# GpSimd's scatters and gathers wait for the landing of the two transfers of the tile two in front, not for all behind each eight

## The reference

```
x = x + tanh(g_xattn) * attention(layernorm(x), ctx)      # 16 heads of 16
x = x + tanh(g_ffn) * (moe(xf) + shared(xf))              # xf = layernorm(x)

# moe: 16 experts, 2 for each token
logits = xf @ Wg;  gates = softmax over the 2 largest of logits
y = sum over the 2 chosen e of gate_e * ((silu(xf @ W1[e] + b1[e]) * (xf @ W11[e] + b11[e])) @ W2[e] + b2[e])
# shared: the same form with 1024 hidden columns, for all tokens
z = (silu(xf @ Ws1 + bs1) * (xf @ Ws11 + bs11)) @ Ws2 + bs2
```

## Time and profile before

| | |
|---|---|
| median of 3 runs | 604.57 us (603.31 to 604.68) |
| profiled execution, its own time | 601.22 us |
| its span, first to last instruction | 599.5 us |
| mean granted clock of TensorE | 0.983 |
| busy: PE, DVE, ACT, POOL | 556.3, 355.3, 223.2, 345.9 us |
| the 32 scatters | from 219.84 us on |
| the 32 gathers | from 533.30 us on |

### The profile page before, as it was taken

One profiled execution on the slowest core, in us unless ns is written; L12 is line 12 of the kernel. 1 busy time (PEld: TensorE's weight loads), 2 busy tenths in 40 slices (PEclk: granted clock), 3 DMA queues, 4 the chain that ended last, 5 costly groups with the idle time before them and its releaser, 6 DMA issues.

```text
span 599.5 us, 11874 instructions
## 1 busy us (share of the span) xinstructions
PE 556.3 (93%) x3212; PEld 442.9 (74%) x3213; DVE 355.3 (59%) x856; ACT 223.2 (37%) x756; POOL 345.9 (58%) x294
## 2 busy tenths in 40 slices
PE   5789999999976899988899999999999999999995
PEld 4356666566654788867788888888888888888884
DVE  5559778778746562224555566665555555535685
ACT  0687877777756211120222222222222122232331
POOL 4577899899768546672444674464474460236660
PEclk9899999999988899999999999999999999999998
DMA  7572000001020152232455687557557210012224
GB/s 254 205 295 81 28 27 24 21 26 35 10 80 18 48 226 92 93 108 85 175 188 195 232 297 246 201 199 263 191 192 291 88 53 27 28 60 85 85 80 141
DMA packets 32321, 76.07 MB, mean 127 GB/s; under 512 B 4896, under 2 KB 21408, under 8 KB 29344
## 3 DMA queue, kind: packets, MB, share of 16 engines
q1 hardware_dynamic: 12944, 51.52, 23.9%
q10 hardware_dynamic: 16272, 15.74, 8.4%
q0 software_dynamic: 3072, 8.39, 4.4%
HBM read 54.93 MB, written 18.61 MB: 123 GB/s over the span
## 4 chain that ended last, share of the span: by engine, by line
PE 80%; DVE 6%; POOL 5%; issue 4%; ACT 2%; DMA 1%; another core or an unknown queue 1%; DVEq 0%; SPq 0%; ACTq 0%; POOLq 0%
PE mid L674 14%; PE big L655 7%; PE big L657 7%; PE big L656 7%; PE big L574 5%; PE big L572 5%; PE work L425 4%; PE big L573 4%; PE big L454 4%; PE mid L665 3%; POOL arena L1334 2%; PE last L477 2%; PE mid L465 2%; PE work L440 2%; PE work L591 2%
## 5 line engine op out<-in xcount | busy, mean ns | idle before, releaser
L823 ACT ACTIVATE last<-arena 128x512 f32<-128x512 f32 x47 | 28.3, 602 | 184.0 <-DVE arena L1216 184.0
L758 ACT ACTIVATE arena<-big,nmax 128x128 f32<-128x128 f32 x256 | 90.3, 402 | 7.1 <-DVE nmax L939 7.1
L674 PE MATMUL mid<-dring,arena 128*128 x376 | 88.9, 379 | 0.0
L1216 DVE TENSOR_TENSOR arena<-big,bring 128x512 f32<-128x512 f32 x47 | 32.5, 692 | 89.4 <-PE big L657 89.4
L655 PE MATMUL big<-u_hi,xsT_hi 128*128 x188 | 82.4, 438 | 1.6 <-issue 1.6
L1350 POOL TENSOR_TENSOR u_lo<-arena,u_hi 128x2048 fp32r<-128x2048 f32 x16 | 73.3, 4584 | 1.3
L1334 POOL TENSOR_TENSOR arena<-arena,rinv 128x1024 f32<-128x1024 f32 x32 | 60.7, 1896 | 23.2 <-DVE rinv L947 23.2
L657 PE MATMUL big<-u_hi,xsT_lo 128*128 x188 | 73.7, 392 | 0.0
L674 PEld LDWEIGHTS mid<-dring,arena 128*128 128x128 f32 x376 | 67.8, 190 | 7.4
L656 PE MATMUL big<-u_lo,xsT_hi 128*128 x188 | 73.2, 389 | 0.0
L1431 POOL TENSOR_TENSOR pool_mark<-mhalf 128x1 f32<-128x1 f32 x15 | 2.9, 193 | 106.2 <-PE big L657 89.7
(11 more groups left out here) (157 smaller groups left out, 1169.1 us busy)
## 6 DMA issues: line engine op xcount, KB each, us to landing
arena<-up_w_dram SPq DMA_DIRECT2D x16, 1024.0 KB, 7.6
bring<-expert_bias_dram SPq DMA_DIRECT2D x16, 640.0 KB, 5.3
dring<-down_w_dram SPq DMA_DIRECT2D x18, 512.0 KB, 3.4
sorted_y<-arena ACTq DMA_DIRECT2D x47, 128.0 KB, 1.7
arena<-sorted_x ACTq DMA_DIRECT2D x43, 128.0 KB, 2.1
sorted_x<-dring SPq DMA_DIRECT2D x3, 1536.0 KB, 8.6
dring<-up_w_dram SPq DMA_DIRECT2D x2, 1024.0 KB, 4.8
xf_all<-xfs SPq DMA_DIRECT2D x16, 128.0 KB, 2.0
```

Source lines behind the costliest of these rows:

```text
L674: i = mm(mid[:, 1, 0:D], gT[:, p, c, :], dring[:, slot, c * D:(c + 1) * D], start=(c == 0), stop=(c == HC - 1))
L758: i = nc.scalar.activation(probs[:, u % 2, h, :], big[:, u % 2, h // 4, (h % 4) * CTX:(h % 4 + 1) * CTX], ACT.Exp, bias=nmax[:, u % 2, h:h ...
```

## The change

Scatters: in place of the one semaphore `scattered` there are two, one for the even and one for the odd tiles. Before the two transfers of tile t, from tile 2 on, POOL waits until those of tile t-2 have landed, which is all transfers of that parity so far. The wait behind each eight is gone, and nothing on POOL waits for the last tiles' landing any more. SP and ACT wait for both semaphores at 256. Gathers: the same, with `gathered_even` and `gathered_odd` in place of the four semaphores, and `combine(t)` waits for its own tile (`32 * (t // 2 + 1)` of its parity) in place of its group.

```diff
-        scattered = sem("scattered")
+        scattered_even = sem("scattered_even")
+        scattered_odd = sem("scattered_odd")
+        scattered = (scattered_even, scattered_odd)
...
-        gathered = (gathered_0, gathered_4, gathered_8, gathered_12)
+        gathered_even = sem("gathered_even")
+        gathered_odd = sem("gathered_odd")
+        gathered = (gathered_even, gathered_odd)
...
# SP, and in the same way ACT
-            sp.wait_ge(scattered, 16 * TILES * TOPK)
+            for half in scattered:
+                sp.wait_ge(half, 16 * TILES * TOPK // 2)
...
# DVE, combine(t)
-                dve.wait_ge(gathered[t // GROUP], 32 * GROUP)
+                dve.wait_ge(gathered[t % 2], 16 * TOPK * (t // 2 + 1))
...
# POOL, scatters
             for t in range(TILES):
+                if t >= 2:
+                    pool.wait_ge(scattered[t % 2], 16 * TOPK * (t // 2))
                 for k in range(TOPK):
                     g.indirect_dma_start(out=sorted_x, out_offset=bass.IndirectOffsetOnAxis(ap=pos[:, k, t:t + 1], axis=0),
-                                         in_=xf_all[:, t, :], in_offset=None).then_inc(scattered, 16)
-                if t % GROUP == GROUP - 1:
-                    pool.wait_ge(scattered, 16 * TOPK * (t + 1))
+                                         in_=xf_all[:, t, :], in_offset=None).then_inc(scattered[t % 2], 16)
...
# POOL, gathers
             for t in range(TILES):
                 yg = yg_b if t >= GATHERS else yg_a
+                if t >= 2:
+                    pool.wait_ge(gathered[t % 2], 16 * TOPK * (t // 2))
                 for k in range(TOPK):
                     g.indirect_dma_start(out=yg[:, t % GATHERS, k, :], out_offset=None, in_=sorted_y,
                                          in_offset=bass.IndirectOffsetOnAxis(ap=pos[:, k, t:t + 1], axis=0)) \
-                        .then_inc(gathered[t // GROUP], 16)
-                if t % GROUP == GROUP - 1:
-                    pool.wait_ge(gathered[t // GROUP], 16 * TOPK * GROUP)
+                        .then_inc(gathered[t % 2], 16)
```

More of the change, by code:

```diff
@@ L313, in flamingo_layer @@
         bs2_ready = sem("bs2_ready")
-        gathered_0 = sem("gathered_0")
-        gathered_4 = sem("gathered_4")
-        gathered_8 = sem("gathered_8")
-        gathered_12 = sem("gathered_12")
-        gathered = (gathered_0, gathered_4, gathered_8, gathered_12)
+        gathered_even = sem("gathered_even")
+        gathered_odd = sem("gathered_odd")
+        gathered = (gathered_even, gathered_odd)
         combined = sem("combined")
@@ L846, in slot @@
                     store_rows(n - 2, q % 2)
-            act.wait_ge(scattered, 16 * TILES * TOPK)
+            for half in scattered:
+                act.wait_ge(half, 16 * TILES * TOPK // 2)
             load_rows(4, 0)
```

## The result

| | before | changed |
|---|---|---|
| median, 4 runs each on one chip | 603.94 us (601.51 to 604.68) | 649.34 us (648.12 to 652.63) |
| profiled execution, its own time | 601.22 us | 652.63 us |
| its span | 599.5 us | 650.9 us |
| mean granted clock of TensorE | 0.983 | 0.952 |

The account below looks back on a forecast made before the run. PE was taken to bound the kernel (busy 556.3 of 599.5 us, 80% of the chain), so POOL's savings counted 0. The terms summed to 0: 601.22 us profiled stays, median forecast 604.5 us, range 601.8 to 606.8.

Parts of the forecast that it names:

- POOL's rows: Profile forecast: every scatter with 0.30 us in front, last ending near 260.4, SP's load near 262, last gather near 577.
- The fourteen waits: Scatters and gathers on POOL: tile t waits for tile t-2's transfers, landed before being asked for; 0 us.
- Rival A: Scatters on POOL: landings come late or waits empty POOL's pipe, so fourteen waits bite; 612 or about 615 us; chance 0.04.
- the landing of 3.2 us: Scatters: landing estimated from HBM latency under high load, 1.41 + 1.8; each wait would cost 0.4, sum still 604.5.
- a landing beyond 2.82 us: Cover on POOL: tile t-1's two transfers and three gaps take 2.82 us; a wait costs only what exceeds that.
- Rival C: POOL's stretch: it pauses as long in small pieces as in three large ones; time stays 604.6 us; chance 0.06.
- Three waits out of the scatters. -4.2 us on POOL: Scatters: last descriptors end at 260.4 instead of 264.64; nobody was held by them, so 0 us on the kernel.
- the same for the gathers: Gathers: three waits out, some 5.2 us off POOL, last ending about 576.9; combines had not waited, so 0 us.
- Rival B: Scatters' last stretch: their traffic delays DVE and ACT, so ending it earlier gives PE up to 2.0 us, 602.5; chance 0.10.
- The range: Whole kernel: 601.8 to 606.8 us, taking in the faster rival and part of the slower one's 7 us.

Follow-up runs that it names:

- the last experiment: Against the changed kernel, all waits kept: ten small multiplications on POOL behind each eight transfers, at scatters and gathers; 599.16 us, ratio 0.9999.

## Why the prediction was wrong

**What held.** POOL's rows came out as written: 31 gaps of 0.30 us, scatters 4.2 us shorter, SP's load right behind them, gathers from 558.38 to 599.58 with 0.30 us between (41.2 us in place of 48.8: 5.2 for the pauses as forecast, and 2.4 less in making descriptors, of which the cause is not shown). The fourteen waits cost 0, as taken: no landing is a releaser in the changed profile, and putting them in or leaving them out (the change against no waits at all, 1.0796 both) makes no difference. Rival A fell with that: the landing of 3.2 us, estimated from the Trainium skill's latency under high load (DMA: Bandwidth & Descriptors, latency and other measured facts), did not come in the changed profile, since a landing beyond 2.82 us would have shown as a wait. It can come: the wait at 253.51 in the last experiment saw its landing at some 253.2, 3.0 us behind the transfer's descriptors (250.26), and cost POOL 0.4 us once. Rival C was not the case.

**The step that failed** is "Three waits out of the scatters. -4.2 us on POOL", and the same for the gathers: the removed waits were priced only by who waited for the scatters to end. They had a second effect, on engines that wait for nothing of POOL's: they gave PE's signals time to catch up. Measured, the term is +22 us at the scatters and +26 at the gathers, not 0.

**Rival B had the place and not the sign.** It asked whether the scatters hold PE up "in a way that the chain names badly", and pointed to the right 2.0 us at 258 to 269 us. It then took the cause for traffic, so that a shorter stretch would help; with three times as many plain transfers PE lost nothing. The case against it, that PE has no such gap in the first 35 us of the same traffic, was the hint to the opposite: lateness builds up where the breaks are too short, and shows on PE only once both chunks that it can hold are waiting to be taken. Two rows would have told: DVE's tiles 2.9 us apart at 249 to 255, and "remote" as a releaser on one core, where there is no other core that could release anything (in the earlier trace rows it stands as "another core or an unknown queue 1%"). B's gain would have had its sign right for the opposite edit: one pause more takes those 2 us of idle time away, of which some 1 us shows in the runs.

**The range** left this out altogether, because both sides of it were built from who waits for POOL. The two terms hold the clock's share: behind its idle times PE ran at 1.2 GHz for a chunk at the scatters (2.8 us) and for parts of the last stage (5.4 us longer busy). The 1.6 us up to the first scatter and the 1.6 us between the two places are in neither term, and their cause is not shown.

**What stays open** is where the signals are held. The runs show when: in indirect transfers on POOL, the more the denser they stand, with 1024 and with 256 bytes a row, and with no other transfers tried. They show whom: news of PE's work to ACT and DVE, and at the gathers PE's own instructions in the middle of a sum, while ACT to DVE and DVE to PE stay prompt in the same rows. Whether PE sends its signals late or they travel late, the rows do not tell. What the making of descriptors and PE's signals have in common on the chip was not found, and no run here looks at it. Why the gathers' stage of the same code takes 66 us in some executions and 70 in others stays open too. That a transfer's length in rows or another pattern of positions matters was not tried.

## What to carry to other kernels

A wait that nobody needs may still be a pause that others live from; before taking it out, compare when each consumer starts with when its producer's record ends, in the stretches between the waits, and take "remote" or "issue" as a releaser on one core for a question and not for noise. Where GpSimd makes dozens of indirect transfers beside TensorE's work, give it a break: at the scatters some 1.7 us behind every six, or a short piece of other work behind each, were enough; at the gathers only 2.5 us of other work behind each eight was tried with success, and 2.05 us of waiting behind each eight was not always enough. And place the breaks so that the last transfer still lands before it is needed. A saving that is "off the critical path" has a second price to look up: what the engine did to others while it was idle.

## What the runs showed of the hardware

- While POOL made indirect transfers of 0.96 us with 0.30 between them, news of PE's matmuls reached ACT and DVE late: 2.4 us some 15 us into the stretch (DVE at 236.63), 5.6 at 20 us, 21 and 25 for the next two chunks. It cost 20 us of PE per stage. At the gathers PE also stopped four times in the middle of a sum, for 3.7 us.
- A slightly lower rate removed it at the scatters: a start every 1.50 us in place of every 1.27.
- Waits of 2.05 us behind each eight gathers left the last stage at 66 us in nine profiled kernels and at 70 in three.
- 48 us of plain transfers from SP at 249 GB/s, and 51 us from POOL at 0.54 us each, left no trace of it.
- Making the descriptors of an indirect transfer of 128 rows took 0.96 us for 1024 bytes a row and for 256 alike.
- A wait on POOL whose semaphore has already been raised leaves the gap to the next indirect transfer at 0.30 us.
- A multiplication of 128x48 on POOL took 0.25 us in a row of ten, and about 0.30 between two transfers.
